# Turned cross-attention: the second score pass eight waves behind the first, and value products in the waves of the projections

## The reference

```python
q = _split_heads(hidden_states @ q_w.T + q_b)      # 16 heads of 16 values
k = _split_heads(context @ k_w.T + k_b)
v = _split_heads(context @ v_w.T + v_b)
scores = jnp.einsum('bhqd,bhkd->bhqk', q, k) / jnp.sqrt(jnp.float32(HD))
scores = jnp.where(mask, -jnp.inf, scores)
probs = jax.nn.softmax(scores, axis=-1)
ctx = jnp.einsum('bhqk,bhkd->bhqd', probs, v)
```

## Time and profile before

| | |
|---|---|
| time, median of 3 runs | 2543.21 us (2537.09 to 2543.56) |
| profiled execution: its own time, span | 2556.27 us, 2554.4 us |
| TensorE matmul busy | 2292.1 us, 90% of the span |
| TensorE weight load busy | 1858.9 us, 73% |
| VectorE busy | 1709.9 us, 67% |
| ScalarE busy | 1483.3 us, 58% |
| GpSimd busy | 406.1 us, 16% |
| granted TensorE clock, mean | 0.918 |
| waves of layer 0, first to last `maxima` | 34.9 to 480.9 us (224 waves) |
| waves of layer 2 | 1416.6 to 1857.3 us |
| waves of layer 3 | 1978.7 to 2422.3 us |

### The profile page before, as it was taken

How to read it: one execution, slowest core, us unless ns; L and a number is a source line. 1 busy time by engine, 2 the same in 40 slices (tenths; PEclk the granted TensorE clock), 3 DMA queues, 4 the chain that set the end, 5 groups by cost and what they waited for, 6 DMA issues and landing times. The chain is left out here.

```text
span 2554.4 us, 67791 instructions
## 1 busy us (share of the span) xinstructions
PE 2292.1 (90%) x26351; PEld 1858.9 (73%) x26351; DVE 1709.9 (67%) x4076; ACT 1483.3 (58%) x2965; POOL 406.1 (16%) x345
## 2 busy tenths in 40 slices
PE   6999999778999999997567999999964999999948
PEld 4888888676777777775544788888843788888738
DVE  5777777437888888886833677777724677777732
ACT  2666666535777777775013566666631566666621
POOL 2222221002211212210000222222002122222000
PEclk8999999888999999998557899999966899999959
DMA  6677676365343443442032766667512777677426
GB/s 129 108 121 121 120 121 107 56 208 145 106 123 99 106 123 94 111 99 56 1 109 64 133 117 117 117 117 117 88 47 65 128 121 122 119 121 122 73 81 209
DMA packets 149180, 277.47 MB, mean 109 GB/s; under 512 B 31599, under 2 KB 69312, under 8 KB 148941
## 3 DMA queue, kind: packets, MB, share of 16 engines
q1 hardware_dynamic: 148942, 274.13, 52.2%
HBM read 118.86 MB, written 0.33 MB: 47 GB/s over the span
## 5 line engine op out<-in xcount | busy, mean ns | idle before, releaser
L1132 DVE TENSOR_REDUCE L0x_tops<-L0x_m_bank 128x1 f32<-128x448 f32 x448 | 262.5, 618 | 130.8 <-PE L0x_m_bank L904 128.6
L1132 DVE TENSOR_REDUCE L3x_tops<-L3x_m_bank 128x1 f32<-128x448 f32 x448 | 262.7, 618 | 130.5 <-PE L3x_m_bank L904 128.3
L454 ACT ACTIVATE L1x_prob<-L1x_p_s,L1x_neg_max 128x512 f32<-128x512 f32 (+1 forms) x400 | 275.5, 689 | 118.8 <-DVE L1x_neg_max L565 116.2
L1132 DVE TENSOR_REDUCE L2x_tops<-L2x_m_bank 128x1 f32<-128x448 f32 x448 | 262.3, 618 | 121.0 <-PE L2x_m_bank L904 118.9
L560 DVE CUSTOM_DVE_ANT_0 L1x_p_s<-L1x_p_s,L1x_mask 128x512 f32<-128x512 f32 (+1 forms) x400 | 273.5, 684 | 38.0 <-PE L1x_p_s L320 32.5
L1037 ACT ACTIVATE L2x_prob<-L2x_s_bank 128x512 f32<-128x512 f32 x448 | 219.6, 542 | 91.8 <-PE L2x_s_bank L915 90.5
L1037 ACT ACTIVATE L0x_prob<-L0x_s_bank 128x512 f32<-128x512 f32 x448 | 219.6, 542 | 90.0 <-PE L0x_s_bank L915 88.4
L1037 ACT ACTIVATE L3x_prob<-L3x_s_bank 128x512 f32<-128x512 f32 x448 | 219.6, 542 | 89.5 <-PE L3x_s_bank L915 88.3
L329 PE MATMUL L1x_p_t<-net_ident,L1x_prob 128*128 128x128 f32 x1568 | 240.4, 274 | 10.6 <-ACT L1x_probT L175 10.4
L329 PEld LDWEIGHTS L1x_p_t<-net_ident,L1x_prob 128*128 128x128 f32 x1568 | 193.1, 141 | 49.0 <-ACT L1x_probT L175 13.9
L320 PE MATMUL L1x_p_s<-L1x_k_stack,L1x_q_stack 96*128 96x512 f32 (+1 forms) x400 | 183.0, 459 | 1.9 <-DVE L1x_q_stack L544 1.9
(11 more groups left out here) (724 smaller groups left out, 4522.5 us busy)
## 6 DMA issues: line engine op xcount, KB each, us to landing
L0x_k_stack<-L0x_kT SPq DMA_DIRECT2D x336, 112.0 KB, 4.0
L2x_k_stack<-L2x_kT SPq DMA_DIRECT2D x336, 112.0 KB, 4.0
L3x_k_stack<-L3x_kT SPq DMA_DIRECT2D x336, 112.0 KB, 4.0
L1x_k_stack<-L1x_kT SPq DMA_DIRECT2D x288, 128.0 KB, 2.4
L3f_w<-in_L_ffn_w SPq DMA_DIRECT2D x16, 1024.0 KB, 9.3
L0x_ctx<-in_ctxT SPq DMA_DIRECT2D x14, 896.0 KB
L2x_ctx<-in_ctxT SPq DMA_DIRECT2D x14, 896.0 KB
L3x_ctx<-in_ctxT SPq DMA_DIRECT2D x14, 896.0 KB
```

The costliest lines, as they stand in the source:

```text
L454: e.activation(prob[:, h % P_RING, 0:nk], p_s[h % S_RING][:, 0:nk], ACT.Exp, bias=neg_max[:, odd, h:h + 1]).then_inc(sem("exped"), 1)
L1132: e.tensor_reduce(tops[:, b % 2, h, half:half + 1], m_bank[n % RING][:, 0:HALF], AX, ALU.max).then_inc(sem("m_free"), 1)
```

## The change

The second pass runs eight waves behind the first in place of seven. With it u is odd where g is odd, so value products, projections and the turn of the queries all fall in odd waves, and even waves have `maxima` and `scores` alone. The places of `turn_out` and `turn_q` in the rings are moved to where they now come: turn_out after wave 13 of a block (before: 11), turn_q after the scores of u % 4 == 1 (before: u % 4 == 2). turn_out and accumulate move from u % 16 == 4 to 5. Nothing is computed that was not, and no count of instructions changes but for one more turn of the loop.

```diff
-LAG = 7
+LAG = 8
...
-    LAST_G = WAVE_END + LAG + 5
+    LAST_G = WAVE_END + LAG + 6
-    M_BLOCK, M_O = 2 * WAVES + 1, 24
+    M_BLOCK, M_O = 2 * WAVES + 1, 28
     def m_at(g, i):
         k = g % WAVES
-        return g // WAVES * M_BLOCK + 2 * k + i + (k > 11)
+        return g // WAVES * M_BLOCK + 2 * k + i + (k > 13)
...
-    S_GROUP, S_Q = 9, 6
+    S_GROUP, S_Q = 9, 4
     def s_at(u, i):
-        return (u // 4 + 1) * S_GROUP + u % 4 * 2 + i + (u % 4 == 3)
+        return (u // 4 + 1) * S_GROUP + u % 4 * 2 + i + (u % 4 >= 2)
...
-                if u % WAVES == 4 and u > 4:
+                if u % WAVES == 5 and u > 5:
                     turn_out(u // WAVES - 1)
...
-                if u % WAVES == 4 and u > 4:
+                if u % WAVES == 5 and u > 5:
                     accumulate(u // WAVES - 1)
```

## The result

The changed kernel takes 2730.21 us (median of 4 runs, 2724.33 to 2735.91) against 2540.15 us before (2533.70 to 2543.56): a ratio of 1.0749, 95% interval 1.0727 to 1.0772. It is **190 us slower**. The forecast was 2668, with a range of 2610 to 2730, so the direction was right and the size a third too small, with the result at the very edge, 0.21 us outside.

A forecast was written before the change was run, and what follows sets the result against it. TensorE was taken as the bound, busy 379.46 of 380 us. Waits 39.0, copy 6.2, turn -4.3 and extra wave 0.6 made 41.5 us per layer, 125 for three: 2668 us, range 2610 to 2730.

The forecast's parts named there:

- pair A: Waves with u % 4 of 0 and 1, eight scores each: 1.55 us from maxima to next scores, 4.45 in all.
- pair B: Waves with u % 4 of 2 and 3, six scores each: 1.33 us from maxima to next scores, 4.16 in all.
- one of L915 released by ScalarE, about 100 per layer: Expected in the profile after: at every even to odd step a scores load that waits until ScalarE releases its bank.
- rival 3: Gaps bring TensorE's clock from 2.4 to 1.2 GHz, 330 us on top, 3000 us; chance 0.03.
- The turn of the queries: One late turn per block, 0.36 us idle before its load, counted as won: 12 x 0.36, -4.3 us per layer.
- copy_out: At u % 16 == 2, now a short wave: next wave's value products wait 0.48 us, 13 times, +6.2 per layer.
- Fill and end: Scores start and end one wave later: an end wave of 1.1 us against 0.48 saved in wave 7, +0.6 per layer.
- Rival 1: Only VectorE's ring counts, ScalarE gives its bank back in time: 80 us more in all, 2623 us; chance 0.13.
- Rival 2: Odd waves find their banks free, one drain less per pair is left: 40 us less, 2503 us; chance 0.05.
- Rival 4: ScalarE's query work delays short waves' exponentials by 0.2 us, or six-score pairs wait as long as eight-score ones: 2732; chance 0.07.
- The changes of tiling mode: Each change drains TensorE, 0.48 against 0.39 us in the trace; three per pair of waves where before there were four.

The follow-up runs named there:

- before_short_both: Kernel before, with VectorE's maximum over 112 of 448 columns and ScalarE's exponentials over 1 tile of 4 or 3: 2508.34 us, ratio 0.986 to before.
- short_exp: Changed kernel with ScalarE's exponentials reading and writing 1 tile of 4 or 3: 2670.48 us.
- copy_early_pool_held: As copy_early, with POOL's split of the context also held until VectorE has written wave 4's columns (wave 8's in the first block): 2702.12 us.
- copy_early: Changed kernel with ScalarE's copy of the value sums one wave earlier, in the odd wave (u % 16 == 1): 2708.61 us.
- short_top: Changed kernel with VectorE's maximum reading 112 of the 448 columns: 2697.92 us.
- values_even: Changed kernel, still at lag 8, with value products back in the even waves and the copy of their sums a wave earlier: 2551.66 us, ratio 1.0059 to before.
- values_first: Changed kernel with value products ahead of the scores in the odd wave: 2817.64 us, ratio 1.1062 to before.

## Why the prediction was right in kind and too small

- **Bound and mechanism: right.** TensorE was the bound with no waits in the steady part (before_short_both: not a hundredth per four waves). The odd wave's second maxima load waits 0.35 for VectorE in pair A and 0.46 in pair B, and A's scores 0.18 for ScalarE. (The forecast sign "one of L915 released by ScalarE, about 100 per layer" came 61 times: in pair B the wait is hidden behind the maxima load.) The clock stayed at 1.00 from 110 to 500 us, so rival 3 did not happen in this kernel.
- **Pair A and pair B: the step that failed.** The distance to the odd wave's scores was right: 1.55 forecast and measured in A, 1.33 forecast and measured in B. The piece behind it was wrong: "then scores 0.48" and "Then 0.38". Those are distances between first matmuls in a stream, where the loads run under the maxima's products. In pair A the loads start only when ScalarE gives the bank back, so the eight loads themselves are the piece: 0.59, and the values start at 2.14, not 2.03. Pair B was reckoned from ScalarE's bank, but it is VectorE's that decides: its second maxima load is at 1.19, and a maxima product and six scores behind it take 0.68, which gives 1.87 and not 1.71. short_exp shows this, with 1.87 for a far faster ScalarE. That is 0.11 and 0.16 more, together the 0.27 that were missing: the steady four waves, without the copy and the late turn, went from 31.8 / 4 = 7.95 to 36.0 / 4 = 9.0, **+1.05 against +0.78 forecast**, 50 x 0.27 = 13 us per layer. The trace of before had pair A's row: in layer 0's last block the loads behind such a wait start at 469.79, 0.52 long, and the values' first load is at 470.38, 0.59 behind; I read their start and not their length. The timeline of the kernel before, weight loads:

```profile
470.38 0.59 PEld L940 LDWEIGHTS L0x_p_oT<-L0x_prob,L0x_v 128*32 128x32 f32 x24
```

- **The turn of the queries: wrong sign.** I took one late turn (rows 10) for one in every block. In the steady part of layer 0 ten of eleven distances to wave 9 were 8.03 or 8.04, and that one 8.35. After the change POOL's split meets wave 4's columns in 11 of 14 blocks, and the turn of wave 5 is late each time: 0.35 us per block by copy_early_pool_held. Forecast -4.3 per layer, measured about +4.
- **copy_out: right, a quarter too large:** 0.36 per block against 0.48 forecast, shown by copy_early. The copy ends where I had it (values at 2.21, forecast 2.19), but without it the values would start at 1.87 and not at 1.71, by the step above.
- **Fill and end:** forecast +0.6 per layer; the last block, counted at nothing, is 1.6 us longer from turn to turn (7.0 and 7.0 for 6.0 and 6.5, the others the same to 0.1).
- **The sum again:** 50 x 1.05 + 4.7 + 4.2 + 1.6 = 63 per layer where 41.5 stood, 189 for three, and 190 measured. That it meets to 1 us is partly luck: the traces have 57.1, 61.7 and 62.7 from the first turn to the last; layer 0 is the least as its second turn came 8.65 us after the first, and 10.0 in the kernel before. Rival 1 (VectorE's ring alone, 2623) is refuted by short_top for pair A; in pair B it named the right ring, but gave it a gain where there was a loss. Rival 2 (faster) is refuted by the waits. Rival 4's number, 2732, was nearest, but by its own reasons (ScalarE held back by 0.2, or pair B waiting as long as A) it was not what happened.
- **The changes of tiling mode.** The Trainium skill (TensorEngine Tiling (Array Packing), Key Properties) says that each change of tiling mode drains TensorE. The traces agree in kind: the loads stand idle for 0.20 before a projection behind values (297.21) and before maxima behind values (304.53 in values_even) alike, with nothing named that they wait for; that this is the drain itself, no run shows. The changed kernel has one such change less per pair, and pays for it with about 0.5 us of waits.

## What to carry to other kernels

Work out how long a bank is away, from its first product through the read to its release, here about 1.2 us, and compare it with the shortest stretch between two fills of the ring, not with the mean. With three banks filled two at a time a wave of 0.7 us stalled, though its neighbour of 3 us left both readers idle. So balance the work between neighbouring fills before you count mode changes. When two rings can bind, follow each to the same later instruction, and not to its own bank's return: the one that comes back last is not always the one that decides. When pricing a step behind a wait, take its loads' full length, since overlap with what came before is lost with the wait. Look for the piece in a place of the trace where the same sequence already occurs, and read it to its end. And count how often a stall repeats before you multiply it.

## What was not expected of the hardware

- Eight scores loads after a wait hold the next kind of load back by 0.59 us, but in a stream behind two maxima products they add only 0.48 to TensorE's program, as they start 0.11 behind the maxima's first load (304.64 in values_even).
- A VectorE operation on 4 columns of SBUF, 0.17 us alone, took 1.58 us while POOL cast 1792 columns, and ended with it; holding POOL back until VectorE had written its columns removed it.
- In values_first the clock stayed near 1.2 GHz for another 40 us at the start of layer 0 with TensorE busy throughout, and it fell near the stage's end. The gaps of 0.35 and 0.46 us in every pair of the changed kernel's steady waves did not lower it (1.00 from 110 to 500 us).
